# Attention with Strassen-Winograd products between two expert layers: softmax kept in the scores' PSUM bank, low part of C22 on GpSimd, yz copied ahead of C22, another order at the entry of the pair loop

## What is computed

```python
x = x + 0.5 * ffn(layernorm(x))     # 64 experts of rank 16, top 16 of 64 gates by softmax
x = x + attn(layernorm(x))          # 32 heads, dims 128, causal
x = x + 0.5 * ffn(layernorm(x))
# attn: q = h @ wq, k, v = h @ wkv; softmax(q k^T * 192**-0.5, causal) v, then @ wo
```

## Time and profile before

| | |
|---|---|
| median of 3 runs | 1141.93 us (1141.19 to 1142.91) |
| the profiled execution | 1145.13 us, span 1143.2 us |
| busy, share of the span | PE 1092.6 us (96%), PEld 85%, DVE 709.4 (62%), ACT 455.6 (40%), POOL 426.2 (37%) |
| first expert layer and entry | 0 to about 166 us |
| pair loop | about 166 to 1029 us, 55.3 us for each of the pairs 1 to 13 |
| second expert layer | about 1029 us to the end |

### The profile page before, as it was taken

The page is one execution under the profiler, slowest core; times in us unless marked ns, Lnnn a source line. Parts: engine busy times, 40 slices in busy tenths (PEclk is TensorE's granted clock), DMA queues, the critical chain, the costliest instruction groups (busy, mean ns, idle before and its releaser), DMA issues.

```text
span 1143.2 us, 20037 instructions
## 1 busy us (share of the span) xinstructions
PE 1092.6 (96%) x6516; PEld 975.3 (85%) x6516; DVE 709.4 (62%) x1904; ACT 455.6 (40%) x1401; POOL 426.2 (37%) x383
## 2 busy tenths in 40 slices
PE   7999878999999999999999999999999999989998
PEld 7989667889898988888888888888888888978997
DVE  7777655656656575757575657575757575565553
ACT  4112244444444444444444444444444444431111
POOL 5450146343535444344444445353636352010000
PEclk8999999999999999999999999999999999989999
DMA  9400011101010101010201111111011111070000
GB/s 373 193 23 15 1 37 37 56 19 56 18 55 18 55 18 55 18 60 13 73 12 61 32 41 37 37 37 37 37 37 37 37 37 35 2 304 1 28 18 28
DMA packets 13766, 59.67 MB, mean 52 GB/s; under 512 B 1456, under 2 KB 1456, under 8 KB 12720
## 3 DMA queue, kind: packets, MB, share of 16 engines
q1 hardware_dynamic: 13744, 59.38, 14.2%
HBM read 48.63 MB, written 10.75 MB: 52 GB/s over the span
## 4 chain that ended last, share of the span: by engine, by line
PE 82%; DVE 10%; ACT 4%; issue 3%; DMA 1%; POOL 0%; DVEq 0%; SPq 0%; ACTq 0%
PE bank L207 24%; PE bank L209 24%; PE bank L208 24%; DVE prob L719 4%; PE bank L357 3%; PE bank L371 3%; PE bank L347 2%; ACT prob L476 2%; PE bank L248 1%; DVE s7q L741 1%; ACT s7k L431 1%; DVE xa L602 1%; DMA upT_raw<-up_w 1%; PE bank L215 0%; DVE st L594 0%
## 5 line engine op out<-in xcount | busy, mean ns | idle before, releaser
L208 PE MATMUL bank<-wv_hi,xc_lo 128*128 128x256 f32 x512 | 145.2, 284 | 0.0
L209 PE MATMUL bank<-wv_hi,xc_hi 128*128 128x256 f32 x512 | 145.1, 283 | 0.0
L207 PE MATMUL bank<-wv_lo,xc_hi 128*128 128x256 f32 x512 | 145.1, 283 | 0.0
L476 ACT ACTIVATE prob<-prob,nmax 128x128 f32<-128x128 f32 (+1 forms) x256 | 113.5, 445 | 63.3 <-DVE nmax L706 63.3
L853 POOL TENSOR_TENSOR stage_w<-stage_w 128x256 f32<-128x256 f32 x128 | 93.4, 752 | 63.3 <-DMA stage_w<-wqk 60.8
L207 PE MATMUL bank<-xc_lo,wk_hi 128*128 128x512 f32 x224 | 92.4, 412 | 23.2 <-ACT s7k L431 17.9
L719 DVE TENSOR_SCALAR prob<-prob,rinv 128x128 f32<-128x128 f32 (+1 forms) x256 | 108.0, 482 | 0.0
L755 DVE TENSOR_TENSOR x<-bank,x 128x512 f32<-128x512 f32 x128 | 85.2, 685 | 28.1 <-PE bank L209 28.1
L207 PE MATMUL bank<-wo_lo,attT_hi 128*128 128x512 f32 x256 | 100.4, 392 | 0.7 <-DVE attT_lo L589 0.7
L208 PEld LDWEIGHTS bank<-wv_hi,xc_lo 128*128 128x128 f32 x512 | 98.2, 192 | 2.5
L207 PEld LDWEIGHTS bank<-wv_lo,xc_hi 128*128 128x128 f32 x512 | 98.3, 192 | 2.5
(11 more groups left out here) (134 smaller groups left out, 2935.9 us busy)
## 6 DMA issues: line engine op xcount, KB each, us to landing
stage_w<-wqk SPq DMA_DIRECT2D x32, 512.0 KB, 3.3
stage_vo<-wv SPq DMA_DIRECT2D x16, 512.0 KB, 4.5
stage_vo<-wo SPq DMA_DIRECT2D x16, 512.0 KB, 3.2
upT_raw<-up_w SPq DMA_DIRECT2D x4, 544.0 KB, 6.0
keep_up<-upT_hi SPq DMA_DIRECT2D x1, 2176.0 KB, 15.7
keep_up<-upT_lo SPq DMA_DIRECT2D x1, 2176.0 KB, 20.5
upT_hi<-keep_up SPq DMA_DIRECT2D x1, 2176.0 KB, 8.7
upT_lo<-keep_up SPq DMA_DIRECT2D x1, 2176.0 KB, 13.5
```

The costliest lines, as they stand in the source:

```text
L207: nc.tensor.matmul(dst, a_hi, b_lo, start=first, stop=False, skip_group_check=onto)
L208: nc.tensor.matmul(dst, a_lo, b_hi, start=False, stop=False, skip_group_check=onto)
L209: return nc.tensor.matmul(dst, a_hi, b_hi, start=False, stop=last, skip_group_check=onto)
L476: nc.scalar.activation(prob[:, b, a:e], prob[:, b, a:e], ACT.Exp, bias=nmax[:, c:c + 1], scale=-1.0, accum_out=rsum[:, c:c + 1]).then_inc( ...
```

## The change

- The maxima step and the exponentials write the scores' bank (`sp[b]`) instead of `prob`; the normalising reads the bank and writes `prob`. The first exponential of a bank waits for both maxima of that bank.
- The low parts of C22, of q and of k, are made by GpSimd (`pool_c22`) instead of VectorE, with semaphores of their own (`q22_split`, `k22_split`); the counts of `q_split` and `k_split` become three a pair.
- In unit j=2 ScalarE copies yz to s7k before it rounds C22 of q.
- The first split of the first weights of q and of k is made in three slices of 512 columns.
- At the entry: values of half 1 are made before the first scores and not in unit j=0 of pair 0; the second group of values of half 0 goes ahead of m2 of k; DVE and ACT follow this order; on VectorE the sum for C11 of k goes ahead of a combination, and the layer norm of tile 6 ahead of another.

```diff
 def act_exp(act, u):
     for b in range(2):
+        act.wait_ge(s["smax_ready"], 4 * u + 2 * b + 2)
         for i, (a, e) in enumerate(((0, P), (P, 3 * P))):
             c = 2 * b + i
-            act.wait_ge(s["smax_ready"], 4 * u + c + 1)
-            nc.scalar.activation(prob[:, b, a:e], prob[:, b, a:e], ACT.Exp,
+            nc.scalar.activation(sp[b][:, a:e], sp[b][:, a:e], ACT.Exp,
...
 # act_pair, j == 2
+    act_snap7(act, "k", p + 1)
     act_c22(act, "q", p + 1)
-    act_snap7(act, "k", p + 1)
...
 # dve_softmax_max
-    out=prob[:, b, a:e], in0=sp[b][:, a:e], in1=mask[:, a:e], scale=-SCALE,
+    out=sp[b][:, a:e], in0=sp[b][:, a:e], in1=mask[:, a:e], scale=-SCALE,
 # dve_normalise_probs
-    nc.vector.tensor_scalar(prob[:, b, a:e], prob[:, b, a:e], rinv[:, c:c + 1], None,
+    nc.vector.tensor_scalar(prob[:, b, a:e], sp[b][:, a:e], rinv[:, c:c + 1], None,
 # dve_c22
     nc.vector.tensor_tensor(s7[g][:, :], acc[g][:, :], s7[g][:, :], ALU.add)
-    dve_low(dve, g, p, 2, s7[g][:, :])
...
+def pool_w_split_sliced(pool, g):
+    wait_alone(pool, s["w_sum_s"], 4 * KIND[g] + 3)
+    for n, a in enumerate(range(0, S4, 2)):
+        # tensor_copy of tiles a, a+1 to w_hi, a wait for it, subtraction to w_lo
...
+def pool_c22(pool, g, p):
+    pool.wait_ge(s[f"{g}_hi_done"], 4 * p + 3)
+    nc.gpsimd.tensor_tensor(unit_tile(lo_t, g, 2), to_split(s7[g][:, :], g),
+                            unit_tile(hi, g, 2).bitcast(F32), ALU.subtract).then_inc(s[f"{g}22_split"], 1)
...
 # pool_pair, after pool_wo
-    if not (final or last_w):
-        pool_w(pool, "q", p + 2)
+    if final:
+        return
+    if not last_w:
+        pool_w_operands(pool, "q", p + 2)
+        pool_w_split(pool, "q", p + 2, 0)
+    pool_c22(pool, "q", p + 1)
+    if not last_w:
+        pool_w_split(pool, "q", p + 2, 1)
+    pool_c22(pool, "k", p + 1)
...
 # TensorE's entry
     pe_att_transpose(pe, NT - 1)
+    pe_value(pe, 0, 1, 1, wait_bank=False)
     pe_m2(pe, "k", 0)
-    pe_value(pe, 0, 1, 1, wait_bank=False)
+    pe_value(pe, 1, 0, 2)
+    pe.wait_ge(s["xaT_split"], NT)
+    pe_value(pe, 1, 1, 3)
     pe_scores(pe, 0, 0)
...
 # VectorE's entry
     dve_gate_inverse(dve, NT - 1)
+    dve_normalise(dve, NT - 2, 1, x[:, NT - 2, :])
     dve_combined(dve, NT - 3)
-    dve_normalise(dve, NT - 2, 1, x[:, NT - 2, :])
...
     dve_att_transposed_half1(dve, NT - 1)
+    dve_value(dve, 0, 1, 1)
+    dve_c11_sum(dve, "k", 0)
     dve_combined(dve, NT - 1)
-    dve_c11(dve, "k", 0)
-    dve_value(dve, 0, 1, 1)
+    dve_low(dve, "k", 0, 0, yz[:, :])
+    dve_value(dve, 1, 0, 2)
+    dve_value(dve, 1, 1, 3)
```

More of the change, by code:

```diff
@@ L175, in build_macaron @@
             kept upagain_loaded downagain_loaded comb_step comb_hi comb_split
-            wv_hi_s wv_split wo_hi_s wo_split w_sum_s wq_hi_s wk_hi_s wq_split wk_split
+            wv_hi_s wv_split wo_hi_s wo_split w_sum_s wq_hi_s wk_hi_s wpro_hi wq_split wk_split
             qx_ready kx_ready qy_ready ky_ready q_snap k_snap q_sum k_sum
             scores_ready smax_ready exp_done rinv_ready p_ready pT_ready pT_hi_done pT_split
-            q_hi_done q_split k_hi_done k_split
+            q_hi_done q_split q22_split k_hi_done k_split k22_split
             fill_ready v_hi_done fill_done av_ready av_hi_done av_split""".split()
@@ L285, in pe_m1 @@
             if not isinstance(p, int) or p > 0:
-                pe.wait_ge(s[f"{g}_split"], 4 * p)
+                pe.wait_ge(s[f"{g}_split"], 3 * p)
             product(g, acc[g], A11, B11, False).then_inc(s[f"{g}x_ready"], 1)
@@ L290, in pe_m2 @@
             if g == "k":
-                pe.wait_ge(s["q_split"], 4 * p + (2 if not isinstance(p, int) or p > 0 else 1))
+                pe.wait_ge(s["q_split"], 3 * p + (2 if not isinstance(p, int) or p > 0 else 1))
             elif not isinstance(p, int) or p > 0:
-                pe.wait_ge(s["k_split"], 4 * p - 2)
+                pe.wait_ge(s["k_split"], 3 * p - 1)
             product(g, yz, A12, B21, False).then_inc(s[f"{g}y_ready"], 1)
@@ L303, in pe_m7 @@
             else:
-                pe.wait_ge(s[f"{g}_split"], 4 * p + 1)
+                pe.wait_ge(s[f"{g}_split"], 3 * p + 1)
             product(g, yz, S3, T3, False).then_inc(s[f"{g}y_ready"], 1)
@@ L341, in pe_output, with pe_scores @@
             last.then_inc(s["fill_ready"], 1)
-        def pe_scores(pe, u, j):
-            pe.wait_ge(s["q_split"], u + 1)
-            pe.wait_ge(s["k_split"], u + 1)
+        def pe_scores(pe, p, j):
+            for g in "qk":
+                if j == 2:
+                    pe.wait_ge(s[f"{g}22_split"], p + 1)
+                else:
+                    pe.wait_ge(s[f"{g}_split"], 3 * p + (1, 2, 0, 3)[j])
             for b in range(2):
@@ L379, in pe_pair @@
                 if not (first and j == 0):
-                    pe_scores(pe, u, j)
+                    pe_scores(pe, p, j)
                 if not final:
@@ L396, in fill @@
                 def fill(ab):
-                    if j == 0:
+                    if j == 0 and not first:
                         pe_value(pe, 1, ab, used + ab)
@@ L512, in act_snap7 @@
             if not isinstance(p, int) or p > 0:
-                act.wait_ge(s[f"{g}_split"], 4 * p - 1)
+                act.wait_ge(s[f"{g}22_split"], p)
             act_copy(s7[g][:, :], yz[:, :]).then_inc(s[f"{g}_snap"], 1)
@@ L567, in act_pair @@
                         act_c22(act, "k", p + 1)
-                if j == 0 or (j == 2 and not final):
+                if (j == 0 and not first) or (j == 2 and not final):
                     act_value(act, 1 if j == 0 else 0, 0, used)
@@ L724, in dve_low, with dve_c11_sum @@
             lo(unit_tile(lo_t, g, i), to_split(src, g), unit_tile(hi, g, i)).then_inc(s[f"{g}_split"], 1)
-        def dve_c11(dve, g, p):
+        def dve_c11_sum(dve, g, p):
             dve.wait_ge(s[f"{g}y_ready"], 3 * p + 1)
@@ L729, in dve_c11 @@
             nc.vector.tensor_tensor(yz[:, :], yz[:, :], s1[:, :], ALU.add).then_inc(s[f"{g}_sum"], 1)
+        def dve_c11(dve, g, p):
+            dve_c11_sum(dve, g, p)
             dve_low(dve, g, p, 0, yz[:, :])
@@ L871, in pool_w_split @@
                        stage_w[:, a:b, :].rearrange("p i n -> p (i n)"),
-                       s[f"w{g}_hi_s"], 2 * p + part + 1, s[f"w{g}_split"])
+                       s[f"w{g}_hi_s"], 2 * p + part, s[f"w{g}_split"])
+        def pool_w_split_sliced(pool, g):
+            wait_alone(pool, s["w_sum_s"], 4 * KIND[g] + 3)
+            for n, a in enumerate(range(0, S4, 2)):
+                done = 3 * KIND[g] + n + 1
+                nc.gpsimd.tensor_copy(w_hi[g][:, a:a + 2, :].rearrange("p i n -> p (i n)"),
+                                      stage_w[:, a:a + 2, :].rearrange("p i n -> p (i n)")).then_inc(s["wpro_hi"], 1)
+                pool.wait_ge(s["wpro_hi"], done)
+                last = nc.gpsimd.tensor_tensor(w_lo[g][:, a:a + 2, :].rearrange("p i n -> p (i n)"),
+                                               stage_w[:, a:a + 2, :].rearrange("p i n -> p (i n)"),
+                                               w_hi[g][:, a:a + 2, :].rearrange("p i n -> p (i n)").bitcast(F32),
+                                               ALU.subtract)
+            last.then_inc(s[f"w{g}_split"], 1)
+        def pool_c22(pool, g, p):
+            pool.wait_ge(s[f"{g}_hi_done"], 4 * p + 3)
+            nc.gpsimd.tensor_tensor(unit_tile(lo_t, g, 2), to_split(s7[g][:, :], g),
+                                    unit_tile(hi, g, 2).bitcast(F32), ALU.subtract).then_inc(s[f"{g}22_split"], 1)
         def pool_w(pool, g, p):
@@ L994, in _ @@
             pool_w_operands(pool, "q", 0)
-            pool_w_split(pool, "q", 0, 0)
+            pool_w_split_sliced(pool, "q")
             pool_rstd(pool, 2, 1)
@@ L1001, in _ @@
             pool_rstd(pool, 6, 0)
-            pool_w_split(pool, "k", 0, 0)
+            pool_w_split_sliced(pool, "k")
             pool_w_split(pool, "k", 0, 1)
@@ L1007, in _ @@
                 pool_rstd(pool, t, 1)
-            pool_w(pool, "q", 1)
+            pool_w_operands(pool, "q", 1)
+            pool_w_split(pool, "q", 1, 0)
+            pool_c22(pool, "q", 0)
+            pool_w_split(pool, "q", 1, 1)
+            pool_c22(pool, "k", 0)
             pool_pair(pool, 0, first=True)
@@ L1146, in _ @@
             act_att_transposed_half1(act, NT - 1)
+            act_value(act, 0, 1, 1)
             act_combined(act, NT - 1)
             act_c11(act, "k", 0)
-            act_value(act, 0, 1, 1)
+            act_value(act, 1, 0, 2)
+            act_value(act, 1, 1, 3)
             act_exp(act, 0)
```

## The result

| | before | changed |
|---|---|---|
| median, us | 1142.42 (1141.19 to 1143.51, 4 runs) | 1105.12 (1103.9 to 1108.76, 4 runs) |
| profiled execution, span | 1145.13, 1143.2 | 1105.1, 1103.3 |
| TensorE busy | 1092.6 (96%) | 1081.0 (98%) |

The account below looks back on a forecast made before the run. TensorE, busy 96% of the span, was taken to bound the kernel, leaving only idle gaps and low clock to win. Terms summed to -41.4 us: profiled execution 1103.7, median 1100.5 us, 8-in-10 range 1094 to 1109.

Parts of the forecast that it names:

- Step 1: Pairs 1 to 13, unit j=2: the stall from transposes to m4 goes, 1.80 us a pair, -23.4 us.
- Step 2: Softmax in the scores' bank: chain 0.35 us longer, exposed in pair 0 (+0.3) and the last pair (+0.9).
- 3. slices: Prologue: weights split in slices let xa finish in time, ending TensorE's wait and the low clock, -4.1 us.
- 4a: Entry: xa of tile 6 normalised before a combination's low part, wait shrinks, -1.1 us, and clock -1.5 us.
- 4b: Entry: two groups of half-1 values leave pair 0, unit j=0, and fill waits before the first scores, -5.9 us.
- 4c: First scores: without the 4.68 us wait the clock isn't low afterwards, -1.5 us.
- 5. pair 0, j=2: Pair 0, unit j=2: transposes to m4 shorter by 2.85 us, plus 1.5 us of clock, -4.3 us.
- Rival B: Softmax outgrows its slack, latency +1.0 us instead of 0.35, j=1 loses 0.3 in 14 pairs: about 1107 us; chance 0.12.
- C: GpSimd still holds up the normalisation though it reads PSUM; only the wait ahead of m4 goes: about 1109 us; chance 0.05.
- E: Exponentials and maxima writing the bank they read take double, past every slack: slower, about 1210 us; chance 0.02.
- F: No change: time saved in j=2 returns as another wait, the period being set by weights or their loads; chance 0.01.
- D: Clock and entry don't pay, or pair 0 stalls for weights: 4 to 6 us less gain, about 1106; chance 0.10.

Follow-up runs that it names:

- e3_hold: The kernel before, with GpSimd made to wait before the weights of q until unit j=2's probabilities are normalised: 1116.2 against 1144.06 us, ratio 0.9761.
- e1: The kernel before with only ScalarE's order changed in unit j=2, yz copied to s7k ahead of rounding C22 of q: 1121.92 against 1144.06 us, ratio 0.9802.
- e2: The kernel before with only the softmax kept in the scores' bank: 1122.72 against 1144.06 us, ratio 0.9816.
- e6: The changed kernel with softmax back in SBUF and GpSimd waiting for normalisation before weights of q (pair 0: also before wv): 1102.03 us, ratio 0.9629.
- e10_after: The changed kernel itself, run again on another chip: 1104.88 us against 1144.76 before, ratio 0.9651.
- e0: The kernel before, unchanged, traced a second time: span 1143.0 us.
- e9: The kernel before with the new order at the entry alone: 1136.19 us against 1144.49, ratio 0.9933.
- e4: The kernel before with the first weights split in slices and nothing else: 1139.91 against 1144.49 us, ratio 0.9965.
- e8: The changed kernel with the softmax in SBUF for the four units of the last pair alone: 1104.61 us, ratio 0.9639.

## Why the prediction was right, and where it was off

Distances on TensorE, both profiled executions (start to start of the same product):

| step | forecast | measured |
|---|---|---|
| 1. pairs 1 to 13 (measured to the start of pair 15) | -23.4 | -22.8 |
| 2. softmax, pair 0 / last pair | +0.3 / +0.9 | +0.7 / +2.0 |
| 3. slices (with clock) | -4.1 | -4.2 |
| 4a. xa of tile 6 / its clock | -1.1 / -1.5 | -1.1 / -1.6 |
| 4b. values into the entry's gaps | -5.9 | -6.1 |
| 4c. clock at the first scores | -1.5 | -1.5 |
| 4d. m3 of k | -0.8 | -0.7 |
| 5. pair 0, j=2 (with clock) | -4.3 | -4.4 |
| sum | -41.4 | -39.7; the spans differ by 39.9 |

- The mechanism was right: GpSimd's work held up the normalisation, and TensorE waited for what stood behind it. Step 1 was right in size (22.8 of 23.4) and in place, and e3_hold shows its cause. What I hadn't seen is that the order and the bank are substitutes (e1 and e2).
- Step 2 is the one that was mis-sized. The chain from scores to the end of the normalisation grew by 0.68 us, not 0.35. From the traces: the four normalisations take 1.37 us instead of 0.99 undisturbed. I had measured from 1.14, a row with a little of GpSimd in it, and taken 1.2; the 0.07 us that I gave a 256-wide one for reading PSUM is 0.13 (475 against 346 ns). The maxima that write the bank take 0.47 instead of 0.42 with 0.14 instead of 0.08 for the read of the accumulator, and ScalarE's exponentials are 0.05 faster each (444 instead of 495 ns for 256 columns), which I had as a possible gain. In the last pair the transposes come 4.8 us after the scores, where 4.6 was forecast and 4.3 read before. Rival B was thus nearer than its 0.12 said: 0.06 us of slack remain in j=1. The loop lost next to nothing (53.58 against 53.53 us a pair in e3 and e6), but by no more than these 0.06 us.
- The medians moved by 37.3 and the profiled executions by 40.0: that of before lay 2.7 above its median, that of the changed kernel on it. On another chip (e10_after) the medians moved by 39.9. Of the 41 us forecast some 6 were clock, and the low stretches come in some executions only: with the same wait, near 81 us in 3 of 6 traces (before, e0, e1; not e2, e3, e9), near 121 us in 4 of 6 (before, e0, e1, e4; not e2, e3), in pair 0, j=2 in 2 of 4 (before, e0; not e4, e9), and behind the 4.7 us wait in all 6. That the four clock terms of the table agree so well is in part luck: the execution that I read had all four stretches, and that of the changed kernel none. So an average execution may have had less to win than the one that I read; whether that is all of the 2.6 us between the two comparisons wasn't settled.
- C, the hold-up in spite of PSUM, E, doubled operations, and F, a period set by the weights, fell (normalisation 1.37 us, pair 53.58 us). D fell in the profiled execution: the entry paid and the clock stayed full. The rule of the Trainium skill that the prediction cites (SBUF — State Buffer, Who interferes with whom) agrees with the traces: 3.53 us beside GpSimd's work, 0.99 us without it, and 1.37 us beside it with the input in PSUM.

## What to carry over

When a VectorE instruction takes three times its usual length, look at what GpSimd does in that stretch before moving work: making GpSimd wait until a short VectorE step is done (e3, e6) cost nothing here, where GpSimd is busy for some 40% of the span, and gave more than moving the data to PSUM, which lengthens the step for every unit. Read undisturbed lengths from a stretch without GpSimd. And where a low clock follows a stall, look at the traces of several executions before counting that loss as a gain.

## What was not expected of the hardware

- After waits of 2.3 us TensorE's granted clock fell in some executions (0.83 of full over 10 us, 0.50 from 84 to 87 us of the kernel before) and stayed full in others of the same code at the same place (1.00 in e2_softmax and e3_hold). In one execution it fell behind waits of 0.76 and 1.19 us (e8_after_mixed). After the wait of 4.7 us at the first scores it fell in all six traces that have it.
- ScalarE's exponential of 256 columns is 51 ns faster from bank to bank than within SBUF (444 against 495 ns); VectorE's normalisation of 256 columns takes 475 ns from a bank against 346 within SBUF (last pair, the changed kernel and e6).
